# A weight stream on one core: odd pieces cut into five transfers, the last two of eight partitions each

## Time and profile before

| what | value |
|---|---|
| median of 3 runs | 229.99 us (228.32 to 234.5) |
| profiled execution, its own time | 230.86 us |
| its span | 228.7 us |
| PE busy | 217.3 us, 95% of the span |
| DMA moved | 76.99 MB, mean 337 GB/s |

### The profile page before, as it was taken

The page is one execution under the profiler, slowest core; times in us unless marked ns, Lnnn a source line. Parts: engine busy times, 40 slices in busy tenths (PEclk is TensorE's granted clock), DMA queues, the critical chain, the costliest instruction groups (busy, mean ns, idle before and its releaser), DMA issues.

```text
span 228.7 us, 10049 instructions
## 1 busy us (share of the span) xinstructions
PE 217.3 (95%) x4797; PEld 210.8 (92%) x4797; DVE 80.5 (35%) x138; ACT 22.3 (10%) x41; POOL 24.6 (11%) x53
## 2 busy tenths in 40 slices
PE   1999998999999999999999999999999999999894
PEld 1889998999999999799989999999999888999893
DVE  2459838051499731457466500000000000000614
ACT  2523000000020120313051000000000000000001
POOL 2255005400000000010003910000000000000000
PEclk9999999999999999999999999999999999999999
DMA  6999999999989989948981999999999999999202
GB/s 224 381 392 419 426 420 408 398 398 387 393 307 380 388 312 322 386 146 308 335 341 37 391 401 390 384 387 393 393 403 374 388 378 376 386 397 337 110 3 69
DMA packets 12363, 76.99 MB, mean 337 GB/s; under 512 B 2554, under 2 KB 2818, under 8 KB 3108
## 3 DMA queue, kind: packets, MB, share of 16 engines
q1 hardware_dynamic: 11792, 75.95, 85.9%
q10 hardware_dynamic: 532, 0.42, 0.6%
HBM read 75.97 MB, written 0.39 MB: 334 GB/s over the span
## 4 chain that ended last, share of the span: by engine, by line
PE 94%; DMA 2%; issue 1%; DVE 1%; ACT 0%
PE acc L779 81%; PE acc L1026 4%; DMA x_sb<-in_x 2%; PE turn L967 1%; PE side L827 1%; PE side L967 1%; PE side L1026 1%; PE turn L855 1%; DVE stats L504 1%; PE acc L797 1%; PE turn L797 0%; PE turn L871 0%; PE side L838 0%; PE turn L838 0%; PE acc L871 0%
## 5 line engine op out<-in xcount | busy, mean ns | idle before, releaser
L779 PE MATMUL acc<-mean,raw 128*64 128x96 f32 x2048 | 85.5, 246 | 1.4 <-issue 1.4
L779 PEld LDWEIGHTS acc<-mean,raw 128*64 128x64 f32 x2048 | 84.9, 137 | 1.8 <-issue 1.8
L779 PE MATMUL acc<-hT,raw 128*64 128x96 f32 x1024 | 44.7, 247 | 0.2
L779 PEld LDWEIGHTS acc<-hT,raw 128*64 128x64 f32 x1024 | 42.9, 137 | 1.5 <-issue 1.2
L742 DVE TENSOR_TENSOR uT<-acc,uT 128x384 f32<-128x384 f32 x2 | 1.1, 558 | 83.0 <-PE acc L779 83.0
L779 PE MATMUL acc<-qT,raw 128*64 128x96 f32 x512 | 22.0, 246 | 1.0 <-issue 1.0
L779 PEld LDWEIGHTS acc<-qT,raw 128*64 128x64 f32 x512 | 21.4, 137 | 1.3 <-issue 1.3
L779 PE MATMUL acc<-kT,raw 128*64 128x96 f32 x512 | 21.7, 246 | 0.0
L779 PEld LDWEIGHTS acc<-kT,raw 128*64 128x64 f32 x512 | 21.3, 137 | 0.3 <-issue 0.3
L779 PE MATMUL acc<-uT,raw 128*64 128x96 f32 x256 | 13.0, 271 | 0.0
L779 PEld LDWEIGHTS acc<-uT,raw 128*64 128x64 f32 x256 | 12.6, 156 | 0.3 <-ACT uT L408 0.2
(11 more groups left out here) (177 smaller groups left out, 149.7 us busy)
## 6 DMA issues: line engine op xcount, KB each, us to landing
raw<-in_weights SPq DMA_DIRECT2D x136, 512.0 KB, 5.6
raw<-in_weights SPq DMA_DIRECT2D x4, 1024.0 KB, 9.8
x_sb<-in_x SPq DMA_DIRECT2D x1, 192.0 KB, 3.7
x_sb<-in_x ACTq DMA_DIRECT2D x1, 192.0 KB, 3.8
out<-out_rows SPq DMA_DIRECT2D x1, 192.0 KB, 2.1
out<-out_rows ACTq DMA_DIRECT2D x1, 144.0 KB, 2.2
out<-out_rows SPq DMA_DIRECT2D x1, 48.0 KB, 2.5
bias_rows<-in_biases ACTq DMA_DIRECT2D x1, 36.0 KB
```

What stands on the lines that cost most here:

```text
L779: mm = pe.matmul(a[g * HD:(g + 1) * HD, b, c * N:(c + 1) * N], raw[:, s, at:at + HD], moving(k0 + k), start=opens and k0 == 0 and c == 0 a ...
```

## The change

Odd pieces from n = 5 on are moved by five transfers where there were two: the even partitions (64 of them), then every fourth partition from 1 (32), every eighth from 3 (16), every sixteenth from 7 (8), and every sixteenth from 15 (8). The five sets are disjoint and make up all 128 partitions. Even pieces stay at two transfers of 64, pieces 0 to 3 at one of 128. The transfers of eight partitions run on the first eight of the 16 DMA engines, one partition on each, by the change's description; the larger ones on all 16. An engine so moves 4 + 2 + 1 + 1 + 1 = 9 partitions of an odd piece where it is one of the first eight, and 4 + 2 + 1 = 7 where it is one of the last eight; before, 8 on each. `landed` counts the transfers of the list. Everything else, slots and waits too, is as it was. 34 pieces are odd and from 5 on: 5, 7, ..., 71.

```diff
 def transfers(n):
-    return 1 if n < 4 else 2
+    if n < 4:
+        return [slice(0, P)]
+    if n % 2:
+        return [slice(0, P, 2), slice(1, P, 4), slice(3, P, 8), slice(7, P, 16), slice(15, P, 16)]
+    return [slice(j, P, 2) for j in range(2)]

 def landed(n):
-    return 16 * sum(transfers(i) for i in range(n % SLOTS, n + 1, SLOTS))
+    return 16 * sum(len(transfers(i)) for i in range(n % SLOTS, n + 1, SLOTS))
...
-                for j in range(transfers(n)):
-                    part = slice(j, P, transfers(n))
+                for part in transfers(n):
                     sp.dma_start(raw[part, n % SLOTS, :], weights[where, part]).then_inc(raw_landed[n % SLOTS], 16)
```

## The result

The changed kernel took 258.2 us in the median of 4 runs (256.56 to 259.45), the kernel before, measured beside it, 231.09 us. The ratio is 1.126, with a 95% interval of 1.111 to 1.142. The forecast was 232.2 us with a range up to 237.2: the time lies far outside. Some executions of every kernel are disturbed and run longer; the differences in us from here on compare the means of the undisturbed ones, 258.1 against 229.2 us and so 29.0 us here, and need not match medians or ratios to the last us.

What follows compares the result with a forecast made beforehand. PE was taken as the bound, busy for 217.3 of 228.7 us. 230.86 us profiled plus 1.6 us for lateness and 0.6 us before 60 us gave 233.1, or 232.2 us from the median; range 228.4 to 237.2 us.

Steps and rivals of the forecast that it cites:

- Bytes for each engine: DMA engines: the first eight move 17 rows a pair of pieces instead of 16, 5.34 us a pair against PE's 5.32.
- the price of a row: DMA engines: an 8 KB row costs an engine 0.308 us with all backlogged, 0.336 us at 390 GB/s; 0.308 taken.
- SP's issues: SP queue: three more issues an odd piece add 0.3 to 1.8 us, low end at 0.28 us each; waiting covers them.
- What falls behind stays behind: Relations, 120 to 212 us: a late engine's landings grow 0.59 us a pair, giving 8 breaks; +1.6 us taken.
- the pauses in the weights' stream: From 60 to 120 us: PE's other work gives the engines pauses, so the change costs nothing there.
- If PE waits at the starts of pieces, the price of a row is: Sign to watch in PE's waits: waiting at the starts of pieces would show the price of a row wrong.
- The warning that small transfers may cost the engines more than their bytes: DMA engines: the prediction fails upward if small transfers cost more than their bytes; no size given.
- The first eight become the bound: Rival, first eight DMA engines: at 0.336 us a row a pair takes 5.89 us, 237.0 us in all; chance 0.20.
- Hidden: Rival: the first eight need 5.30 to 5.34 us a pair, none falls behind for good, 230.0 us; chance 0.23.
- a gain: Rival: the late engines are in the last eight, lose a row a pair, breaks of 2.07 us go, 227.9 us; chance 0.13.
- The Trainium skill's rule on few and large transfers: Weights' transfers: use one of 128 partitions, below 64 KB one pays mostly overhead; if it held, the bound's time would come.
- The change does what it says: Queue 1: transfers of eight partitions run on eight engines, so it must have 12880 packets, where it had 11792.

Runs made afterwards that it cites:

- e2: Changed kernel with its two transfers of eight partitions made one of 16 (every eighth partition from 7): 254.47 us, ratio 1.108.
- e3: Changed kernel's five transfers of an odd piece, same sizes, each of 64 partitions, the odd partitions cut by columns: 236.93 us, ratio 1.030.
- e4: Kernel before, odd pieces in two transfers of partitions 0 to 63 and 64 to 127 instead of even and odd ones: 344.5 us, ratio 1.480.
- g1: Kernel before plus, for each odd piece from 5 on, a transfer of partitions 3, 7, ..., 31 into a spare tile: 233.49 us, ratio 1.019.
- g2: Kernel before plus, for each odd piece from 5 on, a transfer of every sixteenth partition from 7 into a spare tile: 241.12 us, ratio 1.056.
- f3: Kernel before, fetching only the even partitions from piece 6 on, so half of the weights' bytes: 225.44 us, ratio 0.982.
- f2: Changed kernel with three quarters of the weight matmuls left out, transfers, slots and waits unchanged: 247.52 us, one run.
- f4: Kernel before with every piece in one transfer of 128 partitions: 231.35 us, ratio 1.006.
- e1: Changed kernel with odd pieces in three transfers of 64, 32 and 32 partitions, 8 rows for each engine: 234.17 us, ratio 1.023.
- f1: Kernel before with three quarters of the weight matmuls left out, transfers, slots and waits unchanged: 195.82 us, one run.

## Why the prediction was wrong

**The step that failed** is "Bytes for each engine", and in it the price of a row, "0.308 to 0.336 us". Both bounds came from stretches in which nearly all bytes came in transfers of 64 or 128 partitions. The change doesn't only deal out rows unevenly, it deals them to other engines, and this moved the price: 0.42 us in the mean, 25% over the upper bound and 36% over the value taken. The bounds were bounds for the old layout. I had no row for the new one, and should have said that they might not hold for it. The sum that rested on it, 5.34 us a pair against PE's 5.32, became 6.6 us (2.1 MB at 316 GB/s).

**What the runs showed in its place.** e2 has even bytes and 254.5 us; e3 has five transfers and 236.9; e4 has neither small transfers nor uneven bytes and 344.5; g1 and g2 differ in place alone, by 8.6 us. So it is which rows an engine moves in a transfer that sets the price. Why, stays inferred. That rows of different engines meet at one port is read from the Trainium skill's port map; no run looks at a port, and the count above is what supports it. A rival is untested: in every run a row's place in HBM changes together with its partition in SBUF (`raw[part, ...]` from `weights[where, part]`), so none separates a slow write from a slow read. A run that stores rows in another order in HBM, with the partitions left alone, would.

**SP's issues.** Right in direction: SP still waited 80.1 us in 50 waits, and issues stood in the chain in one place only, at 228 us. The low end was wrong: the median issue is 0.59 us, with five in a row, so one of eight partitions costs what one of 64 does, and the 281 ns of the earlier trace rows were no guide. Single issues took up to 1.66 us, in the kernel before up to 1.39, though the earlier trace rows show 0.60 at most; why is open.

**What falls behind stays behind.** The mechanism was right. Landings grew, to 16.7 us where 7 to 10 had been expected, and breaks came 128 matmuls apart, in the relations and before 60 us; f3 shows that the breaks go when half of the weights' bytes go. The sizes were wrong because they hung on the price of a row: breaks of up to 2.2 us instead of 0.45, 26.4 us in all against some 5. Of these, 6.4 us came before 60 us, where the kernel before had 1.1 and the prediction added 0.6; 14.8 us after 130 us; and 5.2 us in three breaks between 60 and 120 us, which it had costed at nothing because of the pauses in the weights' stream. That a break is PE without instructions was argued from its place in mid-piece and its spacing of 256 instructions, not shown by itself.

**A sign that misled.** "If PE waits at the starts of pieces, the price of a row is" wrong, said the prediction. The price was wrong, and PE waited there for 1.2 us only. It stood still in mid-piece instead, before its weights were late: SP's issue at 158.4 us dates the end of a piece, and the break at 159.60 us comes 1.2 us behind it. In f2, where PE has a quarter of the weights' matmuls, the same transfers do show as 97.9 us of waits for weights. The warning that small transfers may cost the engines more than their bytes pointed the right way; it had no price in the sum.

**The rivals.** "The first eight become the bound" had the consequence right, engines as the bound from a row of 0.307 us on, but for the wrong cause and on all sixteen: with its 0.336 us it stopped at 237.0. "Hidden" and "a gain" fell. The Trainium skill's rule on few and large transfers ("DMA: Bandwidth & Descriptors", Rules for kernel authors), which I put beside the bound, is not what acted in the main: f4 finds one transfer as fast as two, and e3 finds five of the right shape 22 us faster than five of the wrong one. That a row's price could depend on which engine moves it was among none of the rivals.

**The base.** "The change does what it says" held, 12880 packets.

## What to carry to other kernels

When a change cuts a transfer differently, ask first which DMA engine then writes which partitions, and only then how many bytes each has: here five transfers with 30 of 128 rows in other places lost four times as much as five without (29.0 against 6.8 us). Keep one layout for all transfers of a stream; strides of 2 and 4 over all 128 partitions (e1) lost 2.9 us, 64 neighbouring partitions nearly halved the rate. And a DMA share near 1.00 says only that packets were under way: take the engines' rate from a stretch or a run in which nobody else sets the pace (421 GB/s here), and read GB/s beside the share.

## What the runs showed of the hardware that was not expected

- One transfer more for each odd piece costs 2 to 4 us (e1 2.9 us, e3 6.8 us for three), though SP had room. Where this comes from is open, and f4 speaks against a general price: with one transfer less in 68 pieces it gained 0.5 us, within the noise.
- The granted clock fell to 0.80 (a mix of its levels of 1.2 and 2.4 GHz) in 174 to 180 us of the changed kernel, after three breaks of 2 us in 17 us, and was 1.00 again from 186 us on. In f1 and f2, where PE had a quarter of the weights' matmuls, it was 0.61 and 0.59 over the long stretches; in e4 0.90.
- With half of the bytes (f3) the four runs agree within 0.6 us, where those of the kernel before beside it lay between 227.7 and 233.6 us. That its spread comes with the weights' traffic is likely by this, not shown.
